# Output gates in the recurrence's record, applied to a chunk's outputs on GpSimd; expert biases added while mixing

## The chip, the core and the metric

The kernel runs on one core of a Trainium2 chip, written in Bass: every engine has its own list of instructions, and semaphores order them. TensorE (PE) multiplies matrices into PSUM, VectorE (DVE), ScalarE (ACT) and GpSimd (POOL) work on SBUF and PSUM, SyncE (SP) issues DMAs, as ACT and POOL do too. The metric is the device time of one execution in microseconds, less is better.

## The reference, cut to what matters

```python
x = L0_attn_x                                   # (8, 512, 256), f32
xn = layernorm(x)
# attention branch: 16 heads of 16, a recurrence over 512 tokens with a 16x16 state S per head
q, k, v = silu(xn@Wq), l2_norm(silu(xn@Wk)), xn@Wv
gk = log_sigmoid(xn@Wf1@Wf2); a = -k * sigmoid(xn@Wgamma) * exp(gk)
S = S*exp(gk_t); S = S + k_t (a_t.S + v_t); o_t = q_t.S          # token after token
o = o * sigmoid(xn@Wog1@Wog2)                                    # the output gates
s = (layernorm(o) * norm_w) @ Wo
# expert branch: top 2 of 8 experts for each token, weights cw from a softmax
out = sum_e cw[:, e] * (gelu(xn@W1[e] + b1[e]) @ W2[e] + b2[e])  # b2: the second biases
g = silu(layernorm(out) * gamma + beta)
return x + s*g
```

## The kernel before, in words

**Tiles, chunks, pairs.** The 4096 tokens make 32 tiles of 128 rows: tile n holds tokens 16n to 16n+15 of all 8 sequences, and so it is also chunk n of the recurrence. The recurrence lays batch x head over the 128 partitions and takes two tokens at a time, a "pair": 8 pairs a chunk, 256 in all (`two_steps(g)`, g = 0 to 255).

**Records.** For each tile PE projects (L836 to L854), ACT and DVE form f, k, q, a, v, and these go as a record `rec` of 5 x 16 numbers for token and head to `rec_d` in HBM (`spill`, L358); SP loads chunk c of it, turned around, into `rbh` (`load_chunk`, L367), three chunks deep. The output gates, one ACT sigmoid (L661), go to `og_d` by a DMA of their own (L361).

**Order on DVE.** Four tiles first, then chunks 0 to 3, with one further tile's record work in each pair, until the routing (`route`, L1035) at the end of the records. Up to chunk 6 DVE does all of a pair; from chunk 7 (`SHARED`) POOL does the decay (L307) and the products with q (L313, L318, L324), and DVE waits for the decay before L1211. Sums over k give a chunk's outputs `obh` (`sum_row`, L1163).

**Experts.** After the routing POOL scatters the rows to `xs_d` (L499), 39 tiles of 256 rows sorted by expert. PE's loop `expert_tile` does L888, the next tile's transposes L876, and for both halves eight matmuls of L900 and one with a single row of ones and b2 (L902). ACT applies GELU (L709) and scales by the weight (L720). POOL scatters the results to `y_d` (`land`, L527) at places in its list that `LAND0`, `LAND_STEP` and `PAIR_STEP` fix: a tile every LAND_STEP/PAIR_STEP pairs, both halves in pairs that follow each other. A landing waits for its data, with POOL's later decays queued behind it.

**The last stage**, pairs 224 to 255 (`WOVEN` = chunk 28 on), weaves in the output, a tile in each pair s. SP fetches a tile's o and gates (L404 to L406), two pairs ahead; DVE multiplies them (`gate_o`, L1103), takes statistics (L1107), every fourth pair their spread (L1113), POOL the scale (L558); ACT normalizes (L791); PE turns and projects (L950, L956); DVE multiplies by g (`gated`, L1120); POOL adds x (L565). Beside that, for two tiles j at a time: ACT loads y (L749), PE adds the two experts' outputs (`add_experts`, L918), ACT takes moments (L760, L765), POOL their scale (`spreads`, L531, in its list at pair 2j), ACT normalizes (L773), PE turns (L930), ACT SiLU (L781), PE turns back (L940). PE's order for j: add_experts(j+1), turn_y(j), turn_back(j), out_rows of tiles 2j-2 and 2j-1. ACT's: normed(j), moments(j+1), silu_g(j), out_normed and out_turned of both tiles, turned_back(j). At s = 0, 8, 16, 24 SP waits for the outputs of the chunk just finished (L428), loads the next chunk and stores that one's outputs; the last rows of a chunk are summed in the third pair of the next.

Of the kernel before, what the change touches and what calls it, by code (L numbers as in the profile page):

```python
# [6 lines left out]
F32 = mybir.dt.float32  # L7
# [4 lines left out]
P = 128  # L12
# [7 lines left out]
REC = 5 * HD  # L20
A_, F_, K_, Q_, V_ = (HD * n for n in range(5))
# [25 lines left out]
RB = 3  # L47
SHARED = 7
LAND0, LAND_STEP = 390.0, 16.46
PAIR_STEP = 3.83  # L50


def build(nc, x, wq, wk, wv, wgamma, wf1, wf2, wog1, wog2, norm_w, wo,
          wg, bg, w1, b1, w2, b2, gamma, beta, out):
    ctx = ExitStack()
    with ctx:
# [6 lines left out]
        def sem(name):  # L63
# [6 lines left out]
        og_d = nc.dram_tensor("og_d", [NT, P, D], F32, kind="Internal").ap()  # L70
# [41 lines left out]
        ogs = work[:, o1 + 6 * D:o1 + 10 * D].rearrange("p (u n) -> p u n", u=RS)  # L112
        ksq = work[:, o1 + 10 * D:o1 + 11 * D]
# [55 lines left out]
        oTs = xTs  # L169
        sel = gw[:, 0, :, :].rearrange("p t e -> p (t e)")  # L170
        b2_flat = b2_sb[:, :, :].rearrange("a e n -> a (e n)")
        f_on = work[:, 0:FR * D].rearrange("p (u d) -> p u d", u=FR)
        fog, fx, f_sg = (work[:, (FR + n * SL) * D:(FR + (n + 1) * SL) * D].rearrange("p (u d) -> p u d", u=SL)
                         for n in range(3))
# [23 lines left out]
        s_og = sem("s_og")  # L198
# [11 lines left out]
        s_ogd = [sem(f"s_ogd{n}") for n in range(RS)]  # L210
# [10 lines left out]
        s_b1t = sem("s_b1t")  # L221
        s_b1 = sem("s_b1")
# [30 lines left out]
        s_o = sem("s_o")  # L253
        s_od = [sem(f"s_od{n}") for n in range(OB)]
        s_fl = [sem(f"s_fl{n}") for n in range(SL)]
        s_mul = sem("s_mul")
# [25 lines left out]
        N_W, N_C = 10, 9  # L282
# [16 lines left out]
        def shared(g):  # L299
            return g // NP >= SHARED  # L300

# [27 lines left out]
        def _(sp):  # L329
# [21 lines left out]
            sp.dma_start(b2_sb[:, :, :], b2.rearrange("(a e) n -> a e n", a=1)).then_inc(s_c, 16)  # L351
# [4 lines left out]
            sp.wait_ge(s_pool0, 4)  # L356
# [21 lines left out]
            for n in range(NT):  # L378
# [6 lines left out]
                done, at = divmod(n - HEAD + 1, NP)  # L385
# [10 lines left out]
            for u in range(RS):  # L396
                sp.wait_ge(s_ogd[u], 16 * (NT // RS))

            def fetch(n):
# [19 lines left out]
            for s in range((NCH - WOVEN) * NP):  # L419
# [12 lines left out]
            sp.wait_ge(s_o, NCH * RING)  # L432
# [10 lines left out]
        def _(pool):  # L443
# [6 lines left out]
                      channel_multiplier=ZR, allow_small_or_imprecise_dtypes=True).then_inc(s_pool0, 1)  # L450
            pool.memset(ident[:, :], 0.0).then_inc(s_id, 1)
# [115 lines left out]
            def prepare_part(c, part):  # L567

# [7 lines left out]
                qa = rows[:, :, Q_:Q_ + 4 * HD].rearrange("p n (s w) -> p n s w", s=2)[:, :, :, 0:HD]  # L576
                fk = rows[:, :, F_:F_ + 2 * HD].rearrange("p n (s w) -> p n s w", s=2)
# [12 lines left out]
            for g in range(SHARED * NP, T // 2):  # L590
# [11 lines left out]
                if 3 <= g % NP < 6 and g // NP + 1 < NCH:  # L602
                    prepare_part(g // NP + 1, g % NP - 3)
# [15 lines left out]
        def _(act):  # L619
# [16 lines left out]
            def silus(n, u4, first, last):  # L636
# [17 lines left out]
                if not no_record:  # L654
                    act.wait_ge(s_ogd[u4], (n // RS) * 16)
# [4 lines left out]
                act.activation(rec[:, u4, :, F_:F_ + HD], heads(psF[u][:, 0:D]), ACT.Sigmoid).then_inc(s_f, 1)  # L660
# [642 lines left out]
```

## Time and profile before

| | us |
|---|---|
| median of 3 runs (lowest, highest) | 1249.84 (1248.97, 1252.61) |
| the profiled execution, its span | 1244.15, 1242.4 |
| DVE busy | 1160.6 (93%) |
| PE busy | 934.6 (75%) |
| POOL busy | 811.9 (65%) |
| ACT busy | 395.0 (32%) |

Four things are to be read from the profile: the busy time of each engine by stretch of time, who waited for whom, the chain of work that ended last, and single instructions in order of time. Idle time before an instruction is put down to what ended it. Where two instructions of an engine overlap, the distance of their starts is what one costs. A matmul of f32 has two records.

### The profile page before, as it was taken

To read this page: it belongs to the slowest core of one execution; us is meant where nothing else is said; L and a number is where in the kernel's file an instruction comes from. 1 tells how busy PE (TensorE), PEld (TensorE's weight loads), DVE (VectorE), ACT (ScalarE), POOL (GpSimd) and SP (SyncE) were. 2 spreads that over 40 slices of the span, in tenths; PEclk is the share of its full clock that TensorE was granted. 3 is DMA by queue.
4 is the path that set the end of the run, shared out by engine and by line. 5 is a ranking of instruction groups with operands and counts; after the bars stand their busy time and mean duration, and the time that the engine had idled before them with its cause. 6 is when DMAs were issued, how large, how long until landed. Compare 5 with 4: busy or idle time off the path is not lost.

```text
span 1242.4 us, 17665 instructions
## 1 busy us (share of the span) xinstructions
PE 934.6 (75%) x3773; PEld 682.2 (55%) x3774; DVE 1160.6 (93%) x3502; ACT 395.0 (32%) x1047; POOL 811.9 (65%) x902
## 2 busy tenths in 40 slices
PE   5888887100029999999999999999999923567674
PEld 2343343000018888887778788887777823345452
DVE  3799999999999999999999999999999997989882
ACT  3444444200003333333322222332322303454552
POOL 3666666367744777676677777667777765676753
PEclk9798889555559999999999999999999976687776
DMA  5665655553335666666656666666656417355322
GB/s 165 196 215 170 214 181 179 140 192 105 111 93 154 189 191 195 191 195 192 185 170 194 184 179 180 190 190 195 195 165 190 120 38 201 118 152 156 106 81 68
DMA packets 247252, 202.61 MB, mean 163 GB/s; under 512 B 141425, under 2 KB 225233, under 8 KB 247185
## 3 DMA queue, kind: packets, MB, share of 16 engines
q1 hardware_dynamic: 170146, 82.81, 25.3%
q10 hardware_dynamic: 70224, 100.49, 24.3%
q0 software_dynamic: 6816, 18.69, 4.4%
q14 instruction: 56, 0.46, 0.1%
q8 instruction: 10, 0.16, 0.1%
HBM read 139.42 MB, written 62.54 MB: 163 GB/s over the span
## 4 chain that ended last, share of the span: by engine, by line
DVE 53%; issue 16%; PE 15%; DMA 6%; ACT 4%; POOL 3%; SPq 2%; ACTq 0%; DVEq 0%; POOLq 0%
DVE obh L1163 8%; DVE outer L1203 6%; DVE psB L1189 5%; DVE state L1220 5%; PE psA L956 4%; DVE psB L1211 4%; DVE ubuf L1189 4%; PE psF L900 3%; DVE prod_a L1180 3%; DVE ubuf L1191 3%; DMA rec_d<-work 3%; DVE prod_q L1214 3%; PE psF L918 3%; PE psA L888 2%; DVE psB L1199 2%
## 5 line engine op out<-in xcount | busy, mean ns | idle before, releaser
L900 PE MATMUL psF<-wts,work 128*128 128x256 f32 x1248 | 287.6, 383 | 3.2 <-ACT work L709 2.4
L888 PE MATMUL psA<-xgT,wts 128*128 128x256 f32 x1248 | 284.0, 385 | 3.1 <-ACT work L709 2.3
L307 POOL TENSOR_TENSOR decayed<-state,rbh 128x256 f32<-128x256 f32 x200 | 145.5, 727 | 198.3 <-DVE state L1220 177.1
L888 PEld LDWEIGHTS psA<-xgT,wts 128*128 128x128 f32 x1248 | 235.1, 191 | 49.2 <-issue 13.8
L900 PEld LDWEIGHTS psF<-wts,work 128*128 128x128 f32 x1248 | 230.9, 190 | 47.1 <-issue 14.2
L324 POOL TENSOR_TENSOR prod_q<-state,rbh 128x512 f32<-128x512 f32 x175 | 222.8, 1273 | 0.0
L1163 DVE TENSOR_REDUCE obh<-prod_q 128x16 f32<-128x272 f32 x512 | 217.1, 425 | 0.0
L709 ACT ACTIVATE work<-psA,b_sb 128x256 f32<-128x256 f32 x312 | 130.4, 470 | 166.5 <-PE psA L888 158.8
L1180 DVE TENSOR_TENSOR prod_a<-state,psT 128x512 f32<-128x512 f32 x200 | 137.1, 685 | 5.8
L720 ACT ACTIVATE work<-psF,work 128x256 f32<-128x256 f32 x78 | 36.9, 473 | 255.2 <-PE psF L902 252.6
L876 PE MATMUL psT<-ident,work 128*128 128x128 f32 x156 | 24.2, 278 | 120.1 <-DMA work<-xs_d 120.0
L481 POOL TENSOR_TENSOR rinv<-ssm,neghalf 128x16 f32<-128x16 f32 x32 | 100.7, 3148 | 2.7
L499 POOL DMA_INDIRECT xs_d<-x_acc,idx x64 | 79.2, 1237 | 19.5 <-issue 18.9
L1211 DVE TENSOR_TENSOR psB<-decayed,psB 128x256 f32<-128x256 f32 x200 | 83.9, 420 | 5.2 <-POOL decayed L307 5.2
L876 PEld LDWEIGHTS psT<-ident,work 128*128 128x128 f32 x156 | 19.3, 143 | 126.2 <-issue 118.0
L527 POOL DMA_INDIRECT y_d<-work,ids x78 | 78.9, 1012 | 12.6 <-issue 11.4
L1189 DVE TENSOR_REDUCE psB<-prod_a 128x16 f32<-128x272 f32 x200 | 86.5, 432 | 0.0
L1189 DVE TENSOR_REDUCE ubuf<-prod_a 128x16 f32<-128x272 f32 x200 | 85.0, 425 | 0.0
L1201 DVE TENSOR_TENSOR psB<-rbh,psB 128x256 f32<-128x256 f32 x200 | 83.4, 417 | 0.0
L1203 DVE TENSOR_TENSOR outer<-rbh,psB 128x256 f32<-128x256 f32 x200 | 82.4, 412 | 0.0
L1220 DVE TENSOR_TENSOR state<-psB,outer 128x256 f32<-128x256 f32 x200 | 81.8, 409 | 0.0
L842 PE MATMUL psA<-w_kq,xTs 128*128 128x512 f32 x128 | 74.2, 708 | 0.0
(172 smaller groups left out, 1551.3 us busy)
## 6 DMA issues: line engine op xcount, KB each, us to landing
wts<-in_L_ffn_W_dram ACTq DMA_DIRECT2D x78, 1024.0 KB
rec_d<-work SPq DMA_DIRECT2D x32, 640.0 KB
rbh<-rec_d SPq DMA_DIRECT2D x32, 640.0 KB, 4.5
xs_d<-zero SPq DMA_DIRECT2D x26, 387.0 KB, 8.8
work<-xs_d ACTq DMA_DIRECT2D x39, 258.0 KB
wts<-y_d ACTq DMA_DIRECT2D x16, 512.0 KB, 5.5
x_acc<-in_L_attn_x_dram SPq DMA_DIRECT2D x32, 128.0 KB
og_d<-work SPq DMA_DIRECT2D x32, 128.0 KB, 7.8
```

The costliest lines, as they stand in the source:

```text
L307: eng.tensor_tensor(decayed[:, :, :], state[:, g % SR, :, :], over_v(rbh[:, u, 2 * n, F_:F_ + HD]), ALU.mult).then_inc(s_dec, 1)
L324: eng.tensor_tensor(prod_q[:, g % SR, :, :, 0:HD], state[:, g % SR, :, :].unsqueeze(1).broadcast_to(wide), rbh[:, u, 2 * n - 1:2 * n + 1, ...
L481: pool.tensor_tensor(rinv[:, u, :], ssm[:, u, :], neghalf[:, 0:H], ALU.pow).then_inc(s_ng, 1)
L709: act.activation(hT[:, m, :], psA[m // 2 % 2][:, m % 2 * MT:(m % 2 + 1) * MT], ACT.Gelu, bias=b1_sb[:, bass.ds(e * FC + m, 1)]).then_inc(s ...
L888: mm = pe.matmul(psA[m // 2 % 2][:, m % 2 * MT:(m % 2 + 1) * MT], w1_sb[v][:, c, m * P:(m + 1) * P], xgT[:, c, :], start=(c == 0), stop=(c ...
L900: pe.matmul(psF[q][:, 0:D], hT[:, m, q * P:(q + 1) * P], w2_sb[v][:, m, :], start=(m == 0), stop=False)
L1163: dve.tensor_reduce(obh[:, c % OB, row % RING, :], prod_q[:, g % SR, side, :, :], AX.X, ALU.add).then_inc(s_o, 1)
L1180: dve.tensor_tensor(prod_a[:, n, :, :, 0:HD], old.unsqueeze(1).broadcast_to([P, 2, HD, HD]), coef.unsqueeze(2).broadcast_to([P, 2, HD, HD] ...
L1189: dve.tensor_reduce(side, prod_a[:, n, j, :, :], AX.X, ALU.add).then_inc(s_chain, 1)
L1203: dve.tensor_tensor(outer[:, 1, :, :], over_v(rbh[:, u, 2 * n + 1, K_:K_ + HD]), over_k(u2), ALU.mult)\
L1211: dve.tensor_tensor(out1, decayed[:, :, :], out1, ALU.add).then_inc(s_chain, 1)
L1220: dve.tensor_tensor(new, out1, outer[:, 1, :, :], ALU.add).then_inc(s_chain, 1)
```

## The change

1. The record gets a sixth column O, the gates: one sigmoid writes f and the gates, `og_d` and its DMAs go. When a chunk's outputs are complete, they are multiplied by the chunk's O column in place (`gate_outputs`), in the fourth pair of the next chunk (`GATED` = 3): for chunks 0 to 6 on DVE, for 7 to 30 on POOL, for 31 on DVE at the end. Loading a new chunk and storing outputs wait for that. POOL's three parts that prepare a chunk move from pairs 3 to 5 to pairs 4 to 6. DVE's `gate_o` goes.
2. The weights of each token's experts are made into a table in the routing, turned by PE and kept as `cwT` (32 rows for four tiles); `add_experts` begins with a matmul of these with b2 (32 rows, zero but for one tile's 8). The matmul with ones (L902) and PE's load of the expert's number go.
3. `LAND_STEP` 16.46 to 14.7, `PAIR_STEP` 3.83 to 3.86.

```diff
-REC = 5 * HD
-A_, F_, K_, Q_, V_ = (HD * n for n in range(5))
+REC = 6 * HD
+A_, F_, O_, K_, Q_, V_ = (HD * n for n in range(6))
+GATED = 3
-LAND0, LAND_STEP = 390.0, 16.46
-PAIR_STEP = 3.83
+LAND0, LAND_STEP = 390.0, 14.7
+PAIR_STEP = 3.86
-        b2_sb = sb("b2_sb", [1, E, D])
+        b2_sb = sb("b2_sb", [4 * E, 4, D])
...
+        def gate_outputs(eng, c):
+            eng.tensor_tensor(obh[:, c % OB, :, :], obh[:, c % OB, :, :], rbh[:, c % RB, :, O_:O_ + HD], ALU.mult)\
+                .then_inc(s_og, 1)
...
-            sp.dma_start(b2_sb[:, :, :], b2.rearrange("(a e) n -> a e n", a=1)).then_inc(s_c, 16)
+            sp.wait_ge(s_pool0, 5)
+            for n in range(4):
+                sp.dma_start(b2_sb[n * E:(n + 1) * E, n, :], b2).then_inc(s_c, 16)
...
             def spill(n):
-                sp.wait_ge(s_og, n + 1)
-                sp.dma_start(og_d[n], ogs[:, u4, :]).then_inc(s_ogd[u4], 16)
...
             def store_chunk(c):
+                sp.wait_ge(s_og, c + 1)
...
             def next_chunk(c):
-                sp.wait_ge(s_o, (c + 1) * RING)
+                sp.wait_ge(s_og, c + 1)
...
-                done, at = divmod(n - HEAD + 1, NP)
+                done, at = divmod(n - HEAD - GATED, NP)
...
             def fetch(n):
-                    sp.wait_ge(s_mul, n - SL + 1)
+                    sp.wait_ge(s_fb, n - SL + 1)
                 sp.dma_start(f_on[:, n % FR, :], o_r[n]).then_inc(s_fl[n % SL], 16)
-                sp.dma_start(fog[:, n % SL, :], og_d[n]).then_inc(s_fl[n % SL], 16)
...
-                if s % NP == 0:
+                if s % NP == GATED:
                     c = WOVEN + s // NP - 1
-                    sp.wait_ge(s_o, (c + 1) * RING)
+                    sp.wait_ge(s_og, c + 1)
...
+            pool.memset(b2_sb[:, :, :], 0.0).then_inc(s_pool0, 1)
...
-                if 3 <= g % NP < 6 and g // NP + 1 < NCH:
-                    prepare_part(g // NP + 1, g % NP - 3)
+                if g % NP == GATED and g // NP > SHARED:
+                    pool.wait_ge(s_o, g // NP * RING)
+                    gate_outputs(pool, g // NP - 1)
+                if 4 <= g % NP < 7 and g // NP + 1 < NCH:
+                    prepare_part(g // NP + 1, g % NP - 4)
...
-                act.activation(rec[:, u4, :, F_:F_ + HD], heads(psF[u][:, 0:D]), ACT.Sigmoid).then_inc(s_f, 1)
-                act.activation(ogs[:, u4, :], psF[u][:, D:2 * D], ACT.Sigmoid).then_inc(s_og, 1)
+                act.activation(rec[:, u4, :, F_:F_ + 2 * HD].rearrange("p h (s c) -> p s h c", s=2),
+                               psF[u][:, :].rearrange("p (s h c) -> p s h c", s=2, h=H), ACT.Sigmoid).then_inc(s_f, 1)
...
+            act.wait_ge(s_cwT, 1)
+            for n in range(2):
+                act.activation(cwT[:, 4 * n:4 * n + 4, :].rearrange("p n t -> p (n t)"), psA[n][0:4 * E, :], ACT.Copy)\
+                    .then_inc(s_cws, 1)
...
+            pe.wait_ge(s_cw, 1)
+            for n in range(NT // 4):
+                mm = pe.transpose(psA[n // 4][0:4 * E, n % 4 * P:(n % 4 + 1) * P],
+                                  gw[:, 1, 4 * n:4 * n + 4, :].rearrange("p t e -> p (t e)"), ident[:, :])
...
-                e = pe.value_load(etab[0:1, bass.ds(t, 1)], min_val=0, max_val=E - 1)
...
-                    pe.matmul(psF[q][:, 0:D], ones[0:1, :], b2_flat[:, bass.ds(e * D, D)], start=False, stop=True)\
-                        .then_inc(s_y, 1)
+                    mm.then_inc(s_y, 1)
...
                 for n in range(2 * j, 2 * j + 2):
+                    total = sums[j % 2][:, n % 2 * D:(n % 2 + 1) * D]
+                    pe.matmul(total, cwT[:, n // 4, :], b2_sb[:, n % 4, :], start=True, stop=False)
                     for c in range(2):
-                        mm = pe.matmul(sums[j % 2][:, n % 2 * D:(n % 2 + 1) * D], ident[:, :], yab[:, g % YR, c, n % GM, :],
-                                       start=(c == 0), stop=(c == 1))
+                        mm = pe.matmul(total, ident[:, :], yab[:, g % YR, c, n % GM, :], start=False, stop=(c == 1))
...
-                dve.tensor_tensor(x_acc[:, :, D], gs[:, 2, :], gs[:, 0, :], ALU.mult).then_inc(s_gate1, 1)
+                link(dve.tensor_tensor(gs[:, 2, :], gs[:, 2, :], gs[:, 0, :], ALU.mult))
+                dve.tensor_copy(x_acc[:, :, D], gs[:, 2, :]).then_inc(s_gate1, 1)
+                link(dve.tensor_tensor(pr, m1, over_e(2), ALU.mult))
+                link(dve.tensor_tensor(rest_, m2, over_e(4), ALU.mult))
+                dve.tensor_tensor(pr, pr, rest_, ALU.add).then_inc(s_cw, 1)
...
-                if out_tile is not None and out_tile < NT - 1:
-                    gate_o(out_tile)
...
+                    if n == GATED and 0 < c <= SHARED:
+                        dve.wait_ge(s_o, c * RING)
+                        gate_outputs(dve, c - 1)
...
+            dve.wait_ge(s_o, NCH * RING)
+            gate_outputs(dve, NCH - 1)
...
-            gate_o(NT - 1)
```

## Rows read from the trace of the kernel before

**Rows 1.** Busy us of each engine by stretch, granted clock (1.00 is 2.4 GHz), DMA.

```profile
57.00:150.00 93.00, 80.83 (x248) 37.34 (x248) 92.62 (x268) 45.21 (x149) 62.01 (x44) 0.93 0.65 201
...
390.00:1030.00 640.00, 604.64 (x2712) 487.70 (x2710) 634.26 (x1887) 183.36 (x413) 456.01 (x529) 0.98 0.58 176
...
1063.00:1217.00 154.00, 105.44 (x372) 77.38 (x372) 138.07 (x445) 81.25 (x238) 103.59 (x150) 0.74 0.40 117
```

The seven numbers after the length are PE, PEld (weight loads), DVE, ACT, POOL, the clock and the DMA engines' busy share.

**Rows 2.** The chain that ended last: start, length, what; two chunks' first copies.

```profile
446.85 0.81 DVE prod_a L1147
477.76 0.81 DVE prod_a L1147
```

**Rows 3.** Waits from 1020 us on: us in total, times, longest.

```profile
ACT junk L760 <- PE psF L918: 69.9, 15, 36.1
...
DVE work L1120 <- PE psA L956: 18.9, 11, 5.3
...
DVE work L1103 <- DMA work<-og_d: 11.9, 5, 6.9
...
DVE psB L1211 <- POOL decayed L307: 5.2, 4, 1.8
```

**Rows 4.** The chain again, from one L918 to the next.

```profile
1100.98 1.74 PE psF L918 x8
...
1112.99 1.74 PE psF L918 x8
```

**Rows 5.** The chain again: PE L956 of tiles 0, 4, 6 and 26.

```profile
1064.65 2.07 PE psA L956 x4
...
1087.50 1.13 PE psA L956 x4
...
1097.05 2.07 PE psA L956 x4
...
1214.20 2.09 PE psA L956 x4
```

**Rows 6.** Instructions in order of time, from pair 224 on.

```profile
1035.46 0.68 DVE L1180 TENSOR_TENSOR prod_a<-state,psT 128x512 f32<-128x512 f32 x1
...
1039.70 0.68 DVE L1180 TENSOR_TENSOR prod_a<-state,psT 128x512 f32<-128x512 f32 x1
...
1056.24 0.42 DVE L1103 TENSOR_TENSOR work<-work 128x256 f32<-128x256 f32 x1 [6.91 <-DMA work<-og_d]
...
1062.84 0.60 ACT L791 ACTIVATE work<-work,shift,rstd 128x256 f32<-128x256 f32 x1 [7.52 <-POOL shift L560]
```

**Rows 7.** Groups of instructions by shape: busy us, mean ns of one, idle before.

```profile
L307 DVE TENSOR_TENSOR decayed<-state,rbh 128x256 f32<-128x256 f32 x56 | 23.5, 419 | 0.0
...
L583 POOL TENSOR_TENSOR rbh<-rbh 128x256 f32<-128x256 f32 x24 | 17.7, 736 | 0.2
```

**Rows 8.** Instructions in order of time, in the routing.

```profile
247.59 0.42 DVE L1079 COPY tot<-psT 128x256 f32<-128x256 f32 x1 [1.16 <-PE psT L869]
```

**Rows 9.** Waits of the whole span.

```profile
POOL decayed L307 <- DVE psT L1140: 21.1, 1, 21.1
```

**Rows 10.** Instructions of PE in order of time, one expert tile.

```profile
400.54 0.69 PE L902 MATMUL psF<-b_sb,ones 1*128 x2
401.16 7.17 PE L888 MATMUL psA<-xgT,wts 128*128 128x256 f32 x32
...
416.43 0.69 PE L902 MATMUL psF<-b_sb,ones 1*128 x2
```

**Rows 11.** ACT and POOL in order of time: tile 0's output, first and last landing.

```profile
381.10 0.47 ACT L720 ACTIVATE work<-psF,work 128x256 f32<-128x256 f32 x1 [2.56 <-PE psF L902]
...
388.51 1.01 POOL L527 DMA_INDIRECT y_d<-work,ids  x1
...
1024.88 1.01 POOL L527 DMA_INDIRECT y_d<-work,ids  x1 [0.16 <-issue]
```

**Rows 12.** Busy us of each engine in a late turn, behind PE's idle time.

```profile
1188.00:1193.00 5.00, 4.04 (x12) 2.77 (x12) 2.52 (x11) 1.75 (x5) 2.52 (x4) 0.50 0.33 102
```

More of the change, by code:

```diff
@@ L111, in build @@
         f2 = work[:, o1 + 4 * D:o1 + 6 * D].rearrange("p (u n) -> p u n", u=2)
-        ogs = work[:, o1 + 6 * D:o1 + 10 * D].rearrange("p (u n) -> p u n", u=RS)
-        ksq = work[:, o1 + 10 * D:o1 + 11 * D]
+        ksq = work[:, o1 + 6 * D:o1 + 7 * D]
         ss = sb("ss", [P, 2, H])
@@ L169, in build @@
         oTs = xTs
+        cwT = w_kq[0:4 * E, :, :].rearrange("p c n -> p (c n)").rearrange("p (n t) -> p n t", t=P)
         sel = gw[:, 0, :, :].rearrange("p t e -> p (t e)")
-        b2_flat = b2_sb[:, :, :].rearrange("a e n -> a (e n)")
         f_on = work[:, 0:FR * D].rearrange("p (u d) -> p u d", u=FR)
-        fog, fx, f_sg = (work[:, (FR + n * SL) * D:(FR + (n + 1) * SL) * D].rearrange("p (u d) -> p u d", u=SL)
-                         for n in range(3))
+        fx, f_sg = (work[:, (FR + n * SL) * D:(FR + (n + 1) * SL) * D].rearrange("p (u d) -> p u d", u=SL)
+                    for n in range(2))
         s_x = [sem(f"s_x{n}") for n in range(len(STATS))]
@@ L197, in build @@
         s_f = sem("s_f")
-        s_og = sem("s_og")
         s_f2 = sem("s_f2")
@@ L209, in build @@
         s_recd = [sem(f"s_recd{n}") for n in range(RS)]
-        s_ogd = [sem(f"s_ogd{n}") for n in range(RS)]
         s_gt = sem("s_gt")
@@ L221, in build @@
         s_b1t = sem("s_b1t")
+        s_cw = sem("s_cw")
+        s_cwT = sem("s_cwT")
+        s_cws = sem("s_cws")
         s_b1 = sem("s_b1")
@@ L253, in build @@
         s_o = sem("s_o")
+        s_og = sem("s_og")
         s_od = [sem(f"s_od{n}") for n in range(OB)]
         s_fl = [sem(f"s_fl{n}") for n in range(SL)]
-        s_mul = sem("s_mul")
         s_fb = sem("s_fb")
@@ L281, in build @@
         w2_v = w2.rearrange("e (m p) n -> e p m n", p=P)
-        N_W, N_C = 10, 9
+        N_W, N_C = 10, 12
         block = ctx.enter_context(nc.Block())
@@ L395, in _ @@
                 sp.wait_ge(s_yd[u], 16 * MH * ((NM + 1 - u) // 2))
-            for u in range(RS):
-                sp.wait_ge(s_ogd[u], 16 * (NT // RS))
             def fetch(n):
@@ L431, in _ @@
                     store_chunk(c)
-            sp.wait_ge(s_o, NCH * RING)
             store_chunk(NCH - 1)
@@ L574, in both @@
                     return rows[:, :, column:column + HD].unsqueeze(2).broadcast_to(wide)
-                qa = rows[:, :, Q_:Q_ + 4 * HD].rearrange("p n (s w) -> p n s w", s=2)[:, :, :, 0:HD]
-                fk = rows[:, :, F_:F_ + 2 * HD].rearrange("p n (s w) -> p n s w", s=2)
+                qa = rows[:, :, Q_:2 * REC - Q_].rearrange("p n (s w) -> p n s w", s=2)[:, :, :, 0:HD]
+                fk = rows[:, :, F_:2 * K_ - F_].rearrange("p n (s w) -> p n s w", s=2)[:, :, :, 0:HD]
                 if part == 0:
@@ L685, in _ @@
                 act.wait_ge(s_recd[u], 16 * (NT // RS))
-            for u in range(RS):
-                act.wait_ge(s_ogd[u], 16 * (NT // RS))
             def expert_of(t):
@@ L852, in project @@
                 if not first:
-                    pe.wait_ge(s_og, n - 1)
+                    pe.wait_ge(s_f, n - 1)
                 pe.matmul(psF[u][:, :], t1[u][:, :], w_up[:, :], start=True, stop=True).then_inc(s_Fp, 1)
@@ L899, in expert_tile @@
                             pe.wait_ge(s_hb, t * FC + (m + 5))
-                        pe.matmul(psF[q][:, 0:D], hT[:, m, q * P:(q + 1) * P], w2_sb[v][:, m, :],
-                                  start=(m == 0), stop=False)
-                    pe.matmul(psF[q][:, 0:D], ones[0:1, :], b2_flat[:, bass.ds(e * D, D)], start=False, stop=True)\
-                        .then_inc(s_y, 1)
+                        mm = pe.matmul(psF[q][:, 0:D], hT[:, m, q * P:(q + 1) * P], w2_sb[v][:, m, :],
+                                       start=(m == 0), stop=(m == FC - 1))
+                    mm.then_inc(s_y, 1)
             turn_rows(0, 0, 0)
@@ L1099, in route @@
                 dve.tensor_copy(etab[:, :], etab_f[:, :]).then_inc(s_slot, 2)
-            def gate_o(n):
-                dve.wait_ge(s_fl[n % SL], 32 * (n // SL + 1))
-                dve.tensor_tensor(f_on[:, n % FR, :], f_on[:, n % FR, :], fog[:, n % SL, :], ALU.mult).then_inc(s_mul, 1)
             def out_stats(n):
-                dve.wait_ge(s_mul, n + 1)
+                dve.wait_ge(s_fl[n % SL], 16 * (n // SL + 1))
                 dve.bn_stats(stats[:, n, :], f_on[:, n % FR, :]).then_inc(s_fb, 1)
```

5 lines of the change are left out of this document (2 added, 3 removed).

## The prediction

> **What bounds the kernel now.** I read first which engine is full in which stretch of time, then who waited for whom, then the chain that ended last, and only then single instructions. The table by stretches [rows 1] shows VectorE (DVE) busy for 92.6 of 93 us while the records are made and 634.3 of 640 beside the experts. In those stages the recurrence on DVE sets the time. One turn of eight pairs lasts 477.76 - 446.85 = 30.9 us, so 3.863 a pair [rows 2], and no wait of DVE is listed there. TensorE (PE) is nearly as busy beside the experts, but nothing that ends last waits for it.
>
> The last stage, from pair 224 on, is another matter. From 1063 to 1217 us DVE is busy for 138 of 154, and its idle time in the stage is for PE's out product at line 956 (18.9 us), the gate's fetch (11.9) and GpSimd's (POOL's) decay (5.2) [rows 3]. The chain shows why. One turn of it runs: PE L918 (add two tiles' expert outputs), ACT moments (L760, L765) and SiLU (L781), PE L940, then twice PE L950, ACT L798, PE L956, and the next L918. One such turn, between two rows of L918 [rows 4], took 1112.99 - 1100.98 = 12.0 us. DVE is nowhere in it. The first L956 starts at 1064.65 and that of tile 26 at 1214.20: 13 turns in 149.55 us, 11.50 each [rows 5]. PE stands in this ring with every matmul, since it works in order.
>
> Before the ring something else is last. Tile 3's gate waits 6.91 us for its fetch, until 1056.24; the norm scales of tiles 0 to 3 follow, and ACT can normalize tile 0 only at 1062.84 [rows 6]. SyncE (SP) had stood at line 428, waiting for the last rows of a chunk's output, with this fetch queued behind it.
>
> **Part 1: sigma and the record.** The out gate becomes a sixth column. Bytes stay: 128 KB less in its own DMA, 128 KB more in the record's, both ways. ACT does one 128x512 sigmoid instead of two of 256, on an engine that is half idle there. One issue less a tile for SP. In the record stage DVE is full [rows 1], so I cost this at nothing; a slower load of a record would have to eat the eight pairs and more by which it is issued ahead. SP's halt for chunk c's output moves from after tile 8c+11 to after tile 8c+15, when the output is already there; DVE was hardly late for it before, so no gain either.
>
> **Part 2: gating a chunk.** Seven chunks on DVE: a product of 128x256 there lasts 0.42 us [rows 7], so 7 x 0.42 = 2.9 us, plus one at the very end (0.4). Its wait for the chunk's last row is met by an instruction of the pair before, so nothing queues behind it. On POOL 24 products at 0.74 us [rows 7]. It is busy for 456 of 640 us beside the experts, 2.75 a pair of 3.863 [rows 1]; one product in eight pairs adds 0.09 to that. In a pair where it falls beside a landing POOL is full, and ends late by some tenths; DVE needs the decay only before L1211, five instructions into its pair, and never waited for one in that stage. Hidden; behind the waiting POOL would stand the next decay, but the row that it waits for was summed a pair earlier. The prepared parts move one pair later and keep one pair of slack.
>
> **Part 3: routing.** Four DVE steps more and one split in two: 0.2 + 3 x 0.42 = 1.5 us (0.42 as above, the narrow one estimated at half), of which 1.16 fall in DVE's idle time for PE before line 1079 [rows 8]. The end of the routing moves by 0.3 us. The scatter's end moves as much; POOL then has 21.1 us of idle time before its first decay [rows 9]. The transposes of the weights and two ACT copies lie beside the scatter: nothing. The memset and three more small loads of b2 at the start lie beside the first loads: nothing. So pair 224 starts 2.9 + 0.3 = 3.2 us later than its 1035.46 [rows 6].
>
> **Part 4: the expert tiles.** Each has two bias matmuls; from its start to the next instruction one takes 0.62 us (400.54 to 401.16) [rows 10]. An undisturbed tile is 416.43 - 400.54 = 15.89 us, so 14.65 remain. The new steps place a tile every 14.7 / 3.86 = 3.808 pairs, x 3.863 = 14.71 us, where it was 4.298 pairs, 16.60 us, more than PE needed. PE keeps up by 0.06 us a tile, and the first landing is 388.51 - 381.57 = 6.9 us after its data [rows 11]. The last lands at pair 202, near 955, not at 1024.88 [rows 11]. All of this lies beside DVE's 634 busy us: 0, apart from what it does at pair 224 (next part). If a tile took 15.0 instead, POOL would wait at the landings with the decays behind it: 38 x 0.3 - 6.9 = 4 us.
>
> **Part 5: up to the ring.** At pair 224 the experts' outputs are long there; gate and fetch are gone from DVE's pairs. The first pair took 1039.70 - 1035.46 = 4.24 us with a gating of 0.42: 3.8 remain. From pair 227's gating to tile 0's normalizing it was 1062.84 - 1056.24 = 6.6 us, 6.2 without the gating. So from 1038.7: three pairs of 3.8, then 6.2 = 1056.3 instead of 1062.84, **6.5 us earlier** [rows 6]. In that are the 6.91 us of the fetch and the 1.8 that an early pair lost to a late decay [rows 3], POOL having waited for moments that now are long there. The fetch behind SP's later halts is issued in the fourth pair of a chunk for the seventh; DVE's waits for them go too, but the ring doesn't see them.
>
> **Part 6: in the ring.** Every turn now has two more matmuls ahead of the four of L918, 32 rows by 256 columns. The trace has none of this shape there. The nearest rows: L918's own, 1.74 us for four, 0.435 each [rows 4]; and the bias matmul with one row, 0.62 [rows 10], which has the same columns, a weight load of its own and few rows. I take 0.63, since this one also changes the rows in use, 1.26 a turn. Ends: 0.87, and 2.5 if all of it fell in the slow clock. ACT waits for just these matmuls (69.9 us before line 760 in the stage [rows 3]), so nothing hides them. **13 x 1.26 = 16.4 us.**
>
> **Sum.** The tail loses DVE's last gate_o and gains a chunk's gating, 0.42 for 0.42: 0. -6.5 + 16.4 = **+9.9 us**. The profiled execution took 1244.15 with a span of 1242.4: 1254.0 and 1252.3 after. It was 5.7 us below the median of the runs shown, so in their terms 1249.84 + 9.9 = 1259.7.
>
> **The rivals.**
> *The clock pays for it (the other side).* The granted clock in the ring is 0.74 on average: it changes between the levels 1.2 and 2.4 GHz, and in the late turns it is at the lower one after PE has stood idle for ACT's moments and SiLU [rows 1, 12]. The turn from 1087.50 to 1097.05 took 9.55 us, the ten from there on (1214.20 - 1097.05) / 10 = 11.7 [rows 5]. If more work in every turn holds the clock up, a turn is 9.55 + 1.26 = 10.8: 13 x 10.8 = 140.5, 9.0 less than now, with the 6.5 before it 15.5 us in all: 1234. The point from which it decides: 6.5 / 13 = 0.50 us a turn; if the turns grow by less, the change is a gain. For it: the same loop ran a turn in 9.55 us, so the chip does hold the clock for a turn. Against: the idle time under ACT stays whole in every turn, and 1.2 GHz follows it in the late ones [rows 12]. I give this 0.20, and 0.10 to half of it, 1246 to 1253. The Trainium skill, "TensorE: Matmul & The Clock Gate", section "What's actually happening", says that the throttled clock is the default and that activity releases it: more matmuls in each turn are more activity, so by that rule the time would be this rival's. The trace agrees in that the clock isn't at the lower level all the time; which way 1.26 us more would tip a turn, no row shows.
> *DVE was the bound of the last stage.* Then the removed gating (32 x 0.42 = 13.4 us) and its waits (11.9) come off, less 3 [rows 3, 7]: 1228. For it: DVE is busy for 90% of the ring's time. Against: the chain of the ring has no piece of DVE. 0.05.
> *The turns fall worse.* Added work pushes each turn's matmuls further into the slow clock: 2.5 x 13 - 6.5 = +26, 1276. 0.10.
> *Landings stall the decays* (part 4), +4 on top: 1264. 0.05.
>
> **How the numbers follow.** My forecast has 0.50: 13 turns at 0.87 to 1.7 us more (1.26 / 0.74) give +4.8 to +15.6, so 1255 to 1265. Slower by over 0.3% (3.7 us, what a measurement here can tell from none): 0.50 + 0.10 + 0.05 = 0.65. Within: 0.10. Faster: 0.20 + 0.05 = 0.25. The range leaves out the DVE rival and the worst turns, 0.15, and some of the rest beyond its ends: 1234 to 1270.
>
> **What would show it.** Right: expert tiles at 14.65 us and the last landing near 955; DVE still at 30.9 us per eight pairs; pair 224 near 1039; the first L956 near 1058; turns of 12.4 to 13.2 us; more idle time of DVE before line 1120. Wrong: a granted clock well above 0.74 in the ring, turns under 12.0, or DVE in the chain from 1060 on.

## The result and the profile after

The changed kernel takes **1267.17 us** (median of 4 runs, 1264.44 to 1269.9) against 1250.41 (4 runs, 1248.97 to 1252.61): ratio 1.0132, 95% interval 1.0116 to 1.0147, so 16.8 us slower. The forecast was 9.9 us slower, at 1259.7, with a range up to 1270. The profiled execution of the changed kernel took 1264.44 with a span of 1262.7, 20.3 us more than the span before. The rest of this text accounts for those 20.3, since both traces are of single executions.

The first table is the busy time by stretch, as in [rows 1]: length, then PE, PEld, DVE, ACT, POOL, the granted clock, the DMA engines' busy share and GB/s.

```profile
57.00:150.00 93.00, 79.68 (x234) 36.67 (x234) 87.28 (x255) 43.59 (x124) 60.60 (x42) 0.89 0.59 191
390.00:1030.00 640.00, 562.50 (x2597) 481.82 (x2595) 628.42 (x1876) 187.57 (x426) 464.46 (x545) 0.94 0.62 185
1063.00:1217.00 154.00, 110.00 (x384) 72.06 (x384) 116.86 (x382) 73.78 (x219) 93.68 (x138) 0.80 0.36 101
```

Two stretches in which the prediction let nothing change have changed. DVE lost 5.3 busy us in 93 while the records are made (92.62 before) and 5.8 in 640 beside the experts (634.26). In the last stage its load fell from 138 to 117, as the gates left it, and yet the time rose. PE's granted clock there is 0.80 instead of 0.74.

The waits from 1020 us on (us in total, times, longest), beside [rows 3]:

```profile
ACT junk L764 <- PE psF L928: 51.0, 14, 4.1
...
PE psB L949 <- ACT gT L785: 41.6, 16, 3.2
DVE work L1129 <- PE psA L965: 33.0, 17, 5.3
...
DVE psB L1218 <- POOL decayed L311: 24.2, 13, 2.9
```

Line 928 is the old 918, 965 the old 956, 1129 the old 1120 and 1218 the old 1211. The wait for the fetched gate is gone. DVE's wait for the out product grew from 18.9 to 33.0, as forecast; its wait for POOL's decay grew from 5.2 to 24.2, which was not forecast, but DVE isn't what ends last there: it lies in time that DVE would otherwise have spent waiting for PE.

The chain of waits shows a whole turn of the ring, from the sums at 1097.32 to the next sums at 1109.54, behind the out product of 1096.19 (start, length, what; each fp32 matmul leaves two records, so x2 is one matmul; pieces of under 0.25 us are left out). It answers to [rows 4, 5].

```profile
1096.19 1.13 PE psA L965 x4
1097.32 0.62 PE psF L926 x2
1097.94 1.06 PE psF L928 x4
1099.00 0.62 PE psF L926 x2
1099.63 1.07 PE psF L928 x4
1100.72 0.85 ACT junk L764 x4
1102.20 0.65 ACT junk L769 x3
1102.86 0.92 ACT gT L785 x2
1103.82 0.66 PE psB L949 x4
1104.48 0.28 PE psT L959 x2
1104.78 0.39 ACT xTs L802
1105.22 1.89 PE psA L965 x4
1107.11 0.44 PE psT L959 x2
1107.57 0.39 ACT xTs L802
1108.01 1.53 PE psA L965 x4
1109.54 0.62 PE psF L926 x2
```

The new bias matmuls (L926) stand in the chain with 0.62 us each, 1.24 a turn; 1.26 was forecast. The sums as a whole take 1097.32 to 1100.70, 3.4 us, where they took 1.74 before [rows 4]: the two pairs of L928 now take 1.06 each, 2.13 together, 0.4 more than the four in one run did. So the step costs **1.6 us a turn** at 2.4 GHz, not 1.26.

Where the 20.3 us are, each from the starts of the pairs' first copies (L1187, the old L1180) and of the out products:

| | before | after | difference | forecast |
|---|---|---|---|---|
| pair 64 starts | 417.0 | 423.7 | +6.7 | +3.2 |
| pairs 64 to 224 | 618.4 | 622.8 | +4.4 | 0 |
| pair 224 to first out product | 29.2 | 20.3 | -8.9 | -9.7 |
| 13 turns | 149.55 | 166.99 | +17.4 | +16.4 |
| from tile 26's out product to the end | 28.2 | 28.9 | +0.7 | 0 |

### The first loss: a stall of 5 us in the third pair

DVE in order of time (start, length, line, tiles, and in brackets the idle time and what ended it). The rows of 61.90 and 73.90 are the first copies of the third and the fourth pair (g = 2 and 3): 12.0 us, where the kernel before took 6.2. The expectations below call this pair the fourth. At the fourth pair's start the changed kernel is 5.1 us behind the kernel before, and it is still 5.0 behind at pair 28.

```profile
61.90 0.67 DVE L1187 TENSOR_TENSOR prod_a<-state,rbh 128x512 f32<-128x512 f32 x1
...
73.29 0.69 DVE L1019 TENSOR_TENSOR work<-psA,work 128x512 f32<-128x512 f32 x1 [5.69 <-DMA rec_d<-work]
73.90 0.68 DVE L1187 TENSOR_TENSOR prod_a<-state,rbh 128x512 f32<-128x512 f32 x1
```

The chain has the transfer that DVE waited for, the writing of a record to memory:

```profile
62.62 10.58 DMA rec_d<-work
```

Its issue stands late in SP's queue (start, issue time, line, transfer):

```profile
60.65 0.37 SPq L371 DMA_DIRECT2D rbh<-rec_d  x1
61.06 1.45 SPq L388 DMA_DIRECT2D xs_d<-zero  x1
62.62 0.58 SPq L368 DMA_DIRECT2D rec_d<-work  x1
```

In the trace before, the three loads of chunks 0 to 2 were issued at 38.20, 47.62 and 56.95; here at 39.62, 49.92 and 60.65. Each waits for a record's write (768 KB instead of 640), SP stands meanwhile, and between two writes SP issues 387 KB of zeros for the scatter's target (L388). Against before, the loads come 1.4, 2.3 and 3.7 us later, until the record ring has no free slot. The prediction took this change at nothing because the same bytes move; but before, the gate's 128 KB had a transfer and a semaphore of their own, and the load of a chunk did not wait for them.

### The second loss: a landing stall at pairs 176 to 184

One chunk took 36.4 us where the others take 30.9. PE in order of time:

```profile
834.88 7.07 PE L909 MATMUL psF<-wts,work 128*128 128x256 f32 x32
841.78 7.07 PE L898 MATMUL psA<-xgT,wts 128*128 128x256 f32 x32
851.68 0.66 PE L886 MATMUL psT<-ident,work 128*128 128x128 f32 x4 [2.82 <-DMA work<-xs_d]
852.17 8.76 PE L909 MATMUL psF<-wts,work 128*128 128x256 f32 x32
860.77 7.11 PE L898 MATMUL psA<-xgT,wts 128*128 128x256 f32 x32
...
868.15 7.07 PE L909 MATMUL psF<-wts,work 128*128 128x256 f32 x32
...
882.54 7.07 PE L909 MATMUL psF<-wts,work 128*128 128x256 f32 x32
```

An undisturbed tile takes 882.54 - 868.15 = 14.39 us (14.65 were forecast). The one that starts at 834.88 takes 852.17 - 834.88 = 17.29: PE waits 2.82 us for the next tile's rows. It isn't alone: from 390 to 1030 us PE waits 20.7 us in 12 such waits, and the 34 tiles behind the first two take 15.17 us each on average. The plan places one every 14.71, so the landings' data fall further and further behind it. Then the group of L909 behind that wait takes 8.76 us instead of 7.07; the granted clock from 851 to 861 us is 0.83. The rest is a queue of delays: POOL, which must do landings and decays in a set order, waits for the output, and DVE for the decay. POOL and then DVE in order of time:

```profile
858.89 1.01 POOL L528 DMA_INDIRECT y_d<-work,ids  x1 [5.82 <-ACT work L724]
...
873.19 1.01 POOL L528 DMA_INDIRECT y_d<-work,ids  x1 [5.66 <-ACT work L724]
```

```profile
860.89 0.43 DVE L1218 TENSOR_TENSOR psB<-decayed,psB 128x256 f32<-128x256 f32 x1 [2.39 <-POOL decayed L311]
...
875.18 0.43 DVE L1218 TENSOR_TENSOR psB<-decayed,psB 128x256 f32<-128x256 f32 x1 [3.09 <-POOL decayed L311]
```

2.39 + 3.09 = 5.5 us, the whole excess of that chunk. Of POOL's 5.82 + 5.66 = 11.5 us of waiting, half reaches DVE. Two earlier chunks of 30.5 us and a last one without the 0.5 that it lost before give about 1.1 of it back, hence 4.4.

### The profile page after: what moved, and what is told of

Same layout as the page of the kernel before. It is cut to its first block, busy times and chain, and to the rows that moved or that the text cites. A ratio compares the mean times of both kernels' runs of the same rounds, so it can differ in the third digit from the quotient of the medians.

```text
span 1262.7 us, 17186 instructions
## 1 busy us (share of the span) xinstructions
PE 910.4 (72%) x3689; PEld 676.7 (54%) x3689; DVE 1149.8 (91%) x3482; ACT 399.2 (32%) x1017; POOL 827.2 (66%) x927
## 4 chain that ended last, share of the span: by engine, by line
PE 41%; DVE 23%; DMA 12%; issue 9%; POOL 8%; ACT 5%; SPq 1%; ACTq 1%; DVEq 0%; POOLq 0%
PE psF L909 18%; PE psA L898 10%; DMA work<-xs_d 9%; POOL xs_d L500 6%; PE psA L965 4%; DVE obh L1172 3%; PE psF L928 3%; DMA rec_d<-work 2%; DVE outer L1210 2%; DVE state L1227 2%; PE psT L886 2%; DVE psB L1196 1%; PE psF L926 1%; DVE ubuf L1198 1%; DVE prod_a L1187 1%
## 5 line engine op out<-in xcount | busy, mean ns | idle before, releaser
L909 PE MATMUL psF<-wts,work 128*128 128x256 f32 x1248 | 280.5, 384 | 0.0
L898 PE MATMUL psA<-xgT,wts 128*128 128x256 f32 x1248 | 278.9, 382 | 1.5 <-ACT xgT L707 0.8
L909 PEld LDWEIGHTS psF<-wts,work 128*128 128x128 f32 x1248 | 237.5, 193 | 31.7
L1187 DVE TENSOR_TENSOR prod_a<-state,psT 128x512 f32<-128x512 f32 x200 | 137.2, 686 | 6.1
L886 PEld LDWEIGHTS psT<-ident,work 128*128 128x128 f32 x156 | 18.2, 144 | 145.7 <-issue 115.0
L500 POOL DMA_INDIRECT xs_d<-x_acc,idx x64 | 80.0, 1251 | 19.5 <-issue 18.9
L846 PE MATMUL psA<-w_kq,xTs 128*128 128x512 f32 x128 | 77.1, 733 | 0.0
```

What stands on the lines that cost most here:

```text
L500: pool.indirect_dma_start(xs_d, bass.IndirectOffsetOnAxis(idx[:, 2 * n + c:2 * n + c + 1], 0), x_acc[:, n, :], None).then_inc(s_sc, 16)
L898: mm = pe.matmul(psA[m // 2 % 2][:, m % 2 * MT:(m % 2 + 1) * MT], w1_sb[v][:, c, m * P:(m + 1) * P], xgT[:, c, :], start=(c == 0), stop=(c ...
L909: mm = pe.matmul(psF[q][:, 0:D], hT[:, m, q * P:(q + 1) * P], w2_sb[v][:, m, :], start=(m == 0), stop=(m == FC - 1))
L1187: dve.tensor_tensor(prod_a[:, n, :, :, 0:HD], old.unsqueeze(1).broadcast_to([P, 2, HD, HD]), coef.unsqueeze(2).broadcast_to([P, 2, HD, HD] ...
```

## The experiments

"First product" is the start of tile 0's out product, "13 turns" the time from there to tile 26's, "clock" the granted clock in them. Times are medians, spans and the rest of the one profiled execution.

| kernel | time us | ratio to before, 95% | pair 64 | pair 224 | first product | 13 turns | clock |
|---|---|---|---|---|---|---|---|
| before | 1247.6 to 1250.4 | | 417.0 | 1035.5 | 1064.7 | 149.6 | 0.75 |
| changed | 1267.17 | 1.0116 to 1.0147 | 423.7 | 1046.5 | 1066.8 | 167.0 | 0.80 |
| biases_in_tiles | 1246.61 | 0.9966 to 0.9994 | 422.0 | 1040.0 | 1062.9 | 150.5 | 0.75 |
| biases_only | 1264.55 | 1.0108 to 1.0183 | 418.9 | 1037.3 | 1065.4 | 166.5 | 0.80 |
| old_steps | 1273.81 | 1.0191 to 1.0230 | 423.5 | 1041.4 | 1071.6 | 165.5 | 0.81 |
| rows_first | 1264.72 | 1.0084 to 1.0145 | 423.8 | 1041.7 | 1061.5 | 175.3 | 0.73 |
| zero_later | 1257.58 | 1.0051 to 1.0084 | 418.2 | 1039.3 | 1059.6 | 170.4 | 0.77 |
| bias_twice | 1295.84 | 1.0358 to 1.0456 | 423.6 | 1045.7 | 1067.7 | 196.9 | 0.68 |
| sums_in_gap | 1221.27 | 0.9757 to 0.9836 | 423.1 | 1043.5 | 1063.3 | 120.7 | 0.95 |
| before_sums_in_gap | 1241.75 | 0.9944 to 0.9973 | 415.9 | 1034.8 | 1064.8 | 139.0 | 0.79 |
| all_three | 1212.15 | 0.9700 to 0.9735 | 418.7 | 1037.3 | 1059.8 | 116.9 | 0.94 |
| tiles_gap | 1211.69 | 0.9683 to 0.9731 | 417.4 | 1035.4 | 1056.6 | 118.7 | 0.87 |

### Each half of the change alone

**biases_in_tiles** is the changed kernel with the second biases back in the expert tiles and the old planner steps; the gates stay in the record.

```diff
+                    pe.matmul(psF[q][:, 0:D], ones[0:1, :], b2_flat[:, bass.ds(e * D, D)], start=False, stop=True)\
+                        .then_inc(s_y, 1)
...
-                    pe.matmul(total, cwT[:, n // 4, :], b2_sb[:, n % 4, :], start=True, stop=False)
...
-LAND0, LAND_STEP = 390.0, 14.7
+LAND0, LAND_STEP = 390.0, 16.46
```

> The changed kernel with its second part undone: the second biases are added in each expert tile again, the mixing has only its four matmuls, and the landing steps are the old ones; the gates stay in the record. Theory (two more matmuls in every turn of the last stage's ring cost 17.4 of the 20.3 us between the profiled executions): 13 turns from the first out product to that of tile 26 go back from 167.0 to 149.5 us (11.5 each), the stall of the decays behind the landings goes, and the stall near 62 us stays; the span falls from 1262.7 to 1241 to 1246, so level with the kernel before. Rival (the turns are long because the clock fell otherwise, or because the last stage starts with other phases, not by the two matmuls): turns stay at 12.5 us or more and the span at 1255 or more.

**biases_only** is the other half: the kernel before, with the biases added while mixing and the new steps, and nothing of the gates.

> The kernel before with the second biases added while mixing and the new planner steps, and nothing of the gates: the record has five columns, the out gates go through their own buffer, VectorE gates each tile. Theory (the two halves of the change add up): the start is that of the kernel before, pair 64 at 417 us, without the stall in the fourth pair; a landing stall of 3 to 5 us between pairs 128 and 192; 13 turns of the ring at 12.6 to 13.1 us, 164 to 170 in all; time 1264 to 1274 us. Rival (the turns of the changed kernel are longer because VectorE's gating is gone from them and the phases fall otherwise): turns under 12.2 us, time under 1258 us.

The turns follow the biases alone: 150.5 us with the biases in the tiles, 166.5 with them in the mixing, whether the gates have moved or not. Both halves together (1.0146 and 0.998) make the whole (1.0132). The gates' half is worth 0.7 to 4.3 us in all (0.9966 to 0.9994); it would have been more, but DVE's stall at the start comes with it (pair 64 at 422.0, DVE there waits 4.3 us for a record's write). biases_only has some of that stall too, 1.4 us of the same wait: pair 64 at 418.9, not at the expected 417. No run shows why.

biases_only has no landing stall (pairs 64 to 224 in 618.4 us), against its expectation. Its tiles aren't late: PE waits 7.4 us for rows, not 20.7, and a tile takes 14.65 us on average, inside the plan's 14.71. So the late rows come mostly with the gates' half. It moves bytes in time: before, the gates were fetched in the last stage, now they come with the chunks' loads beside the experts, 768 KB each instead of 640, which land after 6.3 us there and after 4.9 in biases_only. But ACT also waits for POOL's row numbers (L518) before it asks for rows, and the gates' half puts work on POOL; which of the two it is wasn't separated.

The stall isn't the same in every execution. With both halves, the new steps and the old order of loads it cost DVE 5.7 us in the changed kernel, 4.0 in zero_later, 4.6 in bias_twice and nothing in sums_in_gap, where one copy on DVE of 2.67 us instead of 0.8 makes up most of what pairs 64 to 224 took over 618. Their tiles took 15.17, 15.15, 15.15 and 14.93 us on average. All four have the same code beside the experts, so one trace without the stall, as of biases_only, doesn't prove that a kernel hasn't got it; PE's shorter wait for rows is the better sign.

### The planner's steps and the two stalls

**old_steps** is the changed kernel with the old steps alone, the first line of the diff above reversed.

> The changed kernel with the old landing steps (16.46 and 3.83). Theory (POOL's landings come too early where TensorE had to wait for its rows, and hold up the decays, 4.4 us): no wait of POOL for the scaled outputs before a landing, eight pairs at 30.9 us throughout, pair 224 at 1042 instead of 1046.5; then 1 to 2 us are given back because the experts' outputs land late again; turns of the ring still at 12.8. Span 1259 to 1262. Rival (the 36.4 us chunk has another cause): it is there again and pair 224 stays at 1046.

The landing stall went (618.0 us from pair 64 to 224), and yet the kernel is slower than the changed one, against its expectation (span 1266.2 instead of 1259 to 1262). The last outputs are now loaded back only at 1034, and the first sums wait for that: the first product starts at 1071.6, 10.1 us later than in rows_first, which has the same pair 224. So the new steps are needed where the biases have left the tiles.

**rows_first** fetches a tile's rows ahead of the 1 MB of second weights:

```diff
-                    load_w2(later, v)
-                if last == 0:
                     act.wait_ge(s_ys, t * MH + (MH + 2))
                     act.wait_ge(s_ids, t + 1)
                     load_rows(t + 2, v)
+                if last == 0:
+                    load_w2(later, v)
```

> The changed kernel, but ACT issues the load of a tile's rows before that of its second weights, not behind it. Theory (the rows' 258 KB stand behind 1 MB of weights in the DMA rings, and now come after TensorE wants them): TensorE's wait for the rows beside the experts falls from 20.7 us to under 5, tiles take 14.4 us, no landing waits, pair 224 at 1042: span 1258. Rival (the DMA engines are simply full, order doesn't matter): the wait stays above 15 us and the span at 1262.

**zero_later** issues the zero fills with tiles 6 to 31 instead of 0 to 25:

```diff
-                if n < ZN:
-                    sp.dma_start(xs_z[n], zero[:, :]).then_inc(s_zero, 16)
+                if 6 <= n < ZN + 6:
+                    sp.dma_start(xs_z[n - 6], zero[:, :]).then_inc(s_zero, 16)
```

> The changed kernel with the 26 fills of the sorted rows' buffer issued with tiles 6 to 31 instead of 0 to 25. Theory (at the start the record's writes, a fifth larger, land after 7.5 to 10.6 us beside the 387 KB fills while SyncE waits for each before it loads the chunk; VectorE then waits 5.7 us at tile 7 for a record buffer): the fourth pair takes 6.2 us again instead of 12.0, and everything after is 5 to 6 us earlier: span 1257. Rival (the larger record alone makes the write slow): the wait stays at 3 us or more.

Both do to their stall what was expected. rows_first takes all of PE's 20.7 us of waiting for rows away, tiles take 14.64 us on average, and the 4.4 us are gone, as in all_three below: the late rows are their cause. Its span of 1264.8 is still not the expected 1258. zero_later brings pair 64 from 423.7 to 418.2, which shows the cause of the other stall: the fills beside the larger writes. But what they give in the end differs: by the ratios (1.0132, then 1.0114 and 1.0067) 2 and 8 us. rows_first reached its first product 5.3 us earlier and lost 8.3 in the 13 turns after it. The table by stretches shows the first two turns of that kernel, the seventh number after the length being the clock:

```profile
1061.00:1078.00 17.00, 13.35 (x33) 8.18 (x32) 13.55 (x43) 6.51 (x20) 11.24 (x17) 0.50 0.30 73
1078.00:1094.00 16.00, 13.21 (x32) 8.18 (x32) 9.79 (x35) 5.71 (x17) 7.11 (x13) 0.50 0.37 115
```

Two turns of 16.5 us ran wholly at 1.2 GHz, as one did in zero_later. PE in order of time in the first of them:

```profile
1066.52 1.22 PE L926 MATMUL psF<-b_sb,w_kq 32*128 32x256 f32 x2
1067.67 2.08 PE L928 MATMUL psF<-wts,ident 128*128 128x256 f32 x4
...
1072.69 1.06 PE L939 MATMUL psT<-ident,wts 128*128 128x128 f32 x4
1076.03 1.11 PE L949 MATMUL psB<-ident,gT 128*128 128x128 f32 x4 [2.27 <-ACT gT L785]
```

Everything of PE takes twice its time, the sums 6.2 us instead of 3.4. So a gain of a few us ahead of the ring can't be counted at its size: in these two traces the ring took back 8.3 and 3.4 us, by the clock that its first turns met.

### What the bias matmuls cost in the ring

**bias_twice** issues each bias matmul of the mixing twice:

```diff
+                    pe.matmul(total, cwT[:, n // 4, :], b2_sb[:, n % 4, :], start=True, stop=True)
                     pe.matmul(total, cwT[:, n // 4, :], b2_sb[:, n % 4, :], start=True, stop=False)
```

> The changed kernel with each bias matmul of the mixing issued twice, the first one's result overwritten; nothing is left out. Theory (each stands in the ring with its own duration): two matmuls more a turn at 0.63 us (2.4 GHz) to 1.15 us for the pair's second half (1.2 GHz), so a turn grows by 0.9 to 1.7 us, 13 turns by 12 to 22 us, time 1279 to 1289 us. Rival (the clock pays for more work in a turn): the granted clock rises above 0.85 in the ring and the turns grow by under 0.5 us; time under 1274 us.

It took 1295.84 us, above both expectations: 13 turns in 196.9, 2.3 us more each than in the changed kernel. The matmuls themselves make 1.24 of it at 2.4 GHz. The rest, 1.1, is left to the clock, which here went the other way than in the rival. The turns alternate between 12.5 and 18.2 us; the first two:

```profile
1067.70:1080.20 12.50, 8.87 (x37) 5.98 (x37) 10.25 (x33) 6.06 (x19) 8.15 (x13) 0.91 0.23 73
1080.20:1098.30 18.10, 14.98 (x36) 9.50 (x36) 10.81 (x39) 6.01 (x19) 8.12 (x13) 0.50 0.33 101
```

PE has the same work in every turn; one of two runs at the lower level throughout. In the changed kernel the turns repeat 13.4, 11.6, 12.8 and 13.3 us. So adding to PE's work raised the clock once (0.75 to 0.80) and lowered it once (0.80 to 0.68).

### Taking the sums out of the ring

**sums_in_gap** lets PE add the outputs of turn j+2 right behind the transposes of turn j, in the time in which it would wait for ACT's SiLU:

```diff
             add_experts(0)
+            add_experts(1)
             for j in range(NT // 2):
-                if j + 1 < NT // 2:
-                    add_experts(j + 1)
                 turn_y(j)
+                if j + 2 < NT // 2:
+                    add_experts(j + 2)
                 turn_back(j)
```

> The changed kernel, but TensorE adds the experts' outputs (with their biases) of turn j+2 right behind the transposes of turn j, while ScalarE is at that turn's moments and SiLU, instead of ahead of turn j+1's work. Theory (the change costs its 1.26 us a turn because the bias matmuls stand in the ring with line 928's four): about 3.0 us (1.26 + 1.74) leave each turn of 12.85, down to what VectorE needs, 124.14 / 13 = 9.55 us a turn at the least; 13 turns in 130 to 140 us instead of 167.0, time 1230 to 1242 us. The start of the kernel and the landing stall stay as in the changed kernel. Rival (the ring isn't made by these matmuls, but by ScalarE and the clock: TensorE idle for longer, then at 1.2 GHz): turns of 12 us and more, time 1257 us and above.

**before_sums_in_gap** is the same edit on the kernel before.

> The same move on the kernel before, where only line 918's four matmuls (1.74 us) move. Theory: a turn falls from 11.50 to VectorE's own need there, 134.95 / 13 = 10.4 us, 13 turns in 135 to 140 us, time 1235 to 1240 us. If so, the changed kernel with the same move lies within 5 us of it, and the change is a matter of where the sums stand. Rival: the turn stays at 11.5 us, because the clock takes back what the move gives; time 1249 us.

**all_three** is the changed kernel with zero_later, rows_first and sums_in_gap together.

> The changed kernel with three edits: the zero fills of the scatter's target are issued with tiles 6 to 31 instead of 0 to 25, an expert tile's rows are fetched ahead of its second weights, and the sums stand in TensorE's gap as in the kernel with that edit alone. Theory: each takes away one of the causes that the traces show. No stall in the fourth pair (5.0 us), no landing stall (4.4 us), and a ring of 130 to 140 us: pair 224 near 1036, time 1220 to 1232 us. Rival (a gain ahead of the ring is given back in it, as with the rows' edit alone, whose first two turns took 16.5 us each at 1.2 GHz): pair 224 near 1036 as well, but the end where the kernel with only the sums moved has it, within 3 us.

**tiles_gap** is biases_in_tiles with zero_later and sums_in_gap.

> The gates as in the changed kernel, but the biases in the expert tiles with the old planner steps, the zero fills issued with tiles 6 to 31, and the sums in TensorE's gap. Beside the kernel with all three edits it asks what the biases' place is worth once the sums have left the ring. Theory (a bias matmul costs only where TensorE is what ends last): VectorE sets the turns at 9.0 to 9.3 us in both, 13 turns in 116 to 121 us; time 1209 to 1216 us, within 4 us of that kernel's 1212.15. Rival (less work for TensorE there is still a gain, since it is busy for 96 of 117 us): 13 turns under 112 us, time under 1207 us. A second rival: outputs that land late, at 1025 us instead of 955, delay the first sums and the ring starts 3 us or more later; time 1216 to 1222 us.

In sums_in_gap the 13 turns fell from 167.0 to 120.7 us, 3.6 each, a little more than the 3.4 that left the chain, and the kernel to 1221, below what was expected (3.0 a turn). all_three, at 1212.15, also came out below both of its expectations, with 13 turns in 116.9 us. One turn of all_three, PE in order of time:

```profile
1085.72 1.13 PE L965 MATMUL psA<-wo_sb,xTs 128*128 128x256 f32 x4 [0.47 <-ACT xTs L802]
...
1088.94 0.66 PE L939 MATMUL psT<-ident,wts 128*128 128x128 f32 x4 [0.27 <-ACT wts L777]
1089.53 0.69 PE L926 MATMUL psF<-b_sb,w_kq 32*128 32x256 f32 x2
1090.15 1.13 PE L928 MATMUL psF<-wts,ident 128*128 128x256 f32 x4
...
1092.80 0.60 PE L949 MATMUL psB<-ident,gT 128*128 128x128 f32 x4
1093.24 0.38 PE L959 MATMUL psT<-ident,work 128*128 128x128 f32 x2
1094.09 1.13 PE L965 MATMUL psA<-wo_sb,xTs 128*128 128x256 f32 x4 [0.47 <-ACT xTs L802]
```

A turn of 8.4 us with the bias matmuls in it. PE no longer waits at L949 (once, 2.3 us, in 13 turns): ACT's moments and SiLU pass under the sums. The stretch of the 13 turns, in the changed kernel and in all_three:

```profile
1066.80:1233.79 166.99, 119.69 (x416) 78.45 (x416) 124.14 (x409) 79.45 (x235) 100.44 (x150) 0.80 0.32 94
```

```profile
1059.76:1176.65 116.89, 96.20 (x405) 62.95 (x405) 115.02 (x383) 78.56 (x235) 94.43 (x138) 0.94 0.45 129
```

PE does the same in 96 busy us instead of 120, since the clock stays up, and DVE is busy for 115.0 of 116.9. DVE is the bound now, and so the gates' half pays at last. The expectation for before_sums_in_gap, to lie within 5 us of sums_in_gap, failed for this reason: its turns fell as expected (139.0), but the whole change is 20 us faster than it, 1221.27 against 1241.75, once both have the sums in the gap. Most of that comes from the gates. before_sums_in_gap, with DVE's gating and its fetches, needs 139.0 us for the turns, 129.9 of them busy on DVE; tiles_gap, with the biases in the same place but without them, 118.7 and 117.3 of them, and 1211.69 in all. Of the 30 us between these two, 20.3 are in the turns and 8.8 between pair 224 and the first product, where the fetch stood. One wait of the former in its 18.1 us turn shows what the gates cost there:

```profile
DVE work L1104 <- DMA work<-og_d: 6.4, 1, 6.4
```

Where the biases are added, however, makes no difference that can be told once the sums stand in the gap: all_three and tiles_gap differ by 0.5 us, inside their intervals. The two also differ in the steps and in the order of loads, so this compares each place with what was best for it. Both are 2.8 to 2.9% faster than the kernel before.

## Why the prediction was right in its sign and short in its size

The time, 1267.2, lies in the range up to 1270, but above the band of 1255 to 1265 that had the chance of 0.50.

- **The bound.** Right. The last stage is a ring of PE and ACT without DVE, each turn carries what is added to PE's matmuls, and biases_in_tiles and biases_only show that nothing else changed the turns.
- **Part 6, the ring.** 12.85 us a turn instead of 11.50, 17.4 in all; 16.4 forecast. The bias matmul was sized right (0.62 against 0.63), but L928's four cost 0.4 more a turn than in one piece, a term that the sum didn't have, and the clock (0.80 for 0.75) would have given some 0.3 back: 1.24 + 0.4 - 0.3 = 1.34. The 0.3 is what is left over, not measured by itself. That the term came out within 1.0 us is in part luck: two things that the sum didn't have nearly cancel.
- **Part 1, the record at no cost.** This step failed, for 5.0 us. It argued that a slower load would have to eat the eight pairs by which it is issued ahead. That holds later; in the first pairs SP waits for a record's write before it may load a chunk, with the next write queued behind. The slack that counts there is the record ring's, and it was used up in three loads.
- **Parts 2 and 3, the gating of chunks and the routing.** Some 1.7 of the 3.2 forecast (6.7 at pair 64 less the stall).
- **Part 4, the expert tiles.** A tile took 14.39 us, under the forecast 14.65, and the last landing was issued at 963.4, not near 955. The rival of the stalled landings came true at its price, 4.4 against 4 (its sum gives 4.5), and by its condition: it asked for tiles of 15.0 us, and with 12 waits for rows they took 15.17 on average, where the plan has 14.71. What the prediction had wrong is that a tile is as long as PE's undisturbed work; it priced no wait for rows. The rival had been given 0.05.
- **Part 5, up to the ring.** From pair 224 the first product came 8.9 us sooner, 9.7 forecast. But pair 224 itself started at 1046.5, not 1038.7, by the two stalls; so of the 6.5 us of gain only a loss of 2.15 was left.
- **The tail.** 0.7 us at the end, not followed up.

The misses add up: 7.9 at pair 224 (5.0 + 4.4, less 1.5 that the gatings and the routing cost less), 0.8 in part 5, 1.0 in part 6, 0.7 at the end, 10.4 us, from 9.9 to 20.3. The medians differ by less, 16.8; two single executions don't settle those 3.5 us.

**The clock rival** was half there: the grant did rise with more work, and by what is left over gave back 0.3 us a turn, where 1.13 of the measured 1.63 were needed to break even (0.50 a turn). Its reason doesn't hold in general, as bias_twice shows. The Trainium skill, "TensorE: Matmul & The Clock Gate", section "What's actually happening", has activity release the throttled clock. The traces agree where PE's idle time is filled (sums_in_gap, 0.80 to 0.95) and don't where work is added beside idle time that stays (bias_twice, 0.80 to 0.68). **The rival with DVE as the bound** was wrong for this kernel and right for the one with the sums moved (DVE busy for 115.0 of 116.9 us).

## What to carry to other kernels

Price an added instruction by where it stands in the ring that ends last, then ask first whether its whole step can move into that ring's idle time: here the same matmuls cost 17 us in one place and nothing that could be told in another. "The same bytes" is no argument that a transfer costs nothing; look at which wait now covers them, and at how full the buffer ring behind it is at its fullest moment. A plan with fixed places is to be checked against the mean of a step with its waits (15.17 us), not against an undisturbed one (14.39). And an engine that waits in every turn is to be relieved of the wait before its work is trimmed: what lies off the path (the gates on DVE) only pays afterwards.

## What the hardware showed that was not expected

- The clock settles into patterns over several turns of identical work: 13.4, 11.6, 12.8, 13.3 in the changed kernel and, from some turn on, in biases_only, old_steps, rows_first and zero_later; 12.5 and 18.2 by turns in bias_twice; first turns of 16.5 at 1.2 GHz in rows_first. By how the first turns fall, 13 turns with the same code in the ring took 165.5 to 175.3 us.
- Behind one wait of PE of 2.82 us, amid dense work, a group of matmuls took 8.76 us instead of 7.07, with a granted clock of 0.83 from 851 to 861 us. Behind another of 2.76 us in the same trace it took 7.07, with 1.00 from 819 to 829.
- The sums' four matmuls took 2.13 us with a bias matmul of 32 rows ahead of each two, 1.74 without. Whether the change of rows or the split makes the 0.4 wasn't tried.
